# A triangular solve on one NeuronCore: the state of the block steps kept in natural layout instead of transposed

## The reference

```python
probs = jax.nn.softmax(logits + causal_mask, axis=-1)      # 16 heads of 8 dims, s = 512
L = jnp.eye(s) - jnp.tril(probs, -1)
rhs = jnp.diagonal(probs, axis1=-2, axis2=-1)[..., None] * v
A = jax.scipy.linalg.solve_triangular(L, rhs, lower=True)
return A.transpose(0, 2, 1, 3).reshape(b, s, 128) @ Wd.T + bd
```

## Time and profile before

| | |
|---|---|
| median of 3 runs | 1500.24 us (1497.93 to 1505.37) |
| profiled execution, span first to last instruction | 1507.1 us, 30851 instructions |
| mean granted TensorE clock, whole span | 0.883 |
| PE busy / DVE busy / ACT busy / POOL busy | 1237.4 / 1035.0 / 729.2 / 628.0 us |
| solve of the causal layer (first inverse to last copy) | 718.5 to 1181.0 us |

### The profile page before, as it was taken

One profiled execution on the slowest core, in us unless ns is written; L12 is line 12 of the kernel. 1 busy time (PEld: TensorE's weight loads), 2 busy tenths in 40 slices (PEclk: granted clock), 3 DMA queues, 4 the chain that ended last, 5 costly groups with the idle time before them and its releaser, 6 DMA issues. The chain is left out here.

```text
span 1507.1 us, 30851 instructions
## 1 busy us (share of the span) xinstructions
PE 1237.4 (82%) x11642; PEld 673.8 (45%) x11642; DVE 1035.0 (69%) x2290; ACT 729.2 (48%) x1596; POOL 628.0 (42%) x838
## 2 busy tenths in 40 slices
PE   6656677779999988538889988988988799999976
PEld 2212232222333337424666766666666333333276
DVE  6699999979888955457446646645632588988653
ACT  3834334317766675313524523533442166676754
POOL 2279888853424215314423423223332524351244
PEclk9878888869999998758889879978997599999988
DMA  5378833023224022441421231141120231331213
GB/s 166 145 274 320 298 139 140 20 67 87 55 65 122 13 82 63 100 86 23 88 38 25 45 74 28 21 100 18 18 51 10 67 79 31 97 89 45 81 48 88
DMA packets 137737, 128.41 MB, mean 85 GB/s; under 512 B 92007, under 2 KB 123559, under 8 KB 132202
## 3 DMA queue, kind: packets, MB, share of 16 engines
q1 hardware_dynamic: 129536, 118.56, 28.6%
q0 software_dynamic: 2496, 5.13, 1.1%
q10 hardware_dynamic: 5558, 2.76, 0.9%
HBM read 105.61 MB, written 38.62 MB: 96 GB/s over the span
## 5 line engine op out<-in xcount | busy, mean ns | idle before, releaser
L1393 DVE TENSOR_REDUCE f_row_min<-f_ps 128x1 f32<-128x512 f32 x512 | 323.9, 676 | 55.6 <-PE f_ps L1720 55.2
L1283 ACT ACTIVATE f_e<-f_ps 128x512 f32<-128x512 f32 x512 | 282.8, 602 | 126.4 <-PE f_ps L1740 122.5
L1720 PE MATMUL f_ps<-f_operands 72*128 72x512 bf16 x512 | 205.4, 410 | 26.4 <-DMA f_operands<-k_scr 15.4
L1740 PE MATMUL f_ps<-f_operands 75*128 75x512 bf16 x512 | 189.5, 380 | 2.6 <-ACT f_e L1283 2.1
L790 PE MATMUL m_ps<-m_shared,sb_ident 128*128 128x512 f32 x256 | 136.8, 683 | 58.1 <-DVE m_shared L630 58.0
L363 POOL TENSOR_TENSOR m_drive<-m_du,m_ring 128x1024 f32<-128x1024 f32 x64 | 149.7, 2352 | 56.2 <-DVE m_ps L622 37.6
L495 ACT ACTIVATE m_ps<-m_delta,m_A 128x511 f32<-128x511 f32 x128 | 83.0, 681 | 131.7 <-DVE m_ps L622 109.0
L1751 PE MATMUL f_ps<-f_e,f_v_op 128*32 128x512 f32 x1024 | 136.4, 604 | 2.1 <-ACT f_e L1283 1.4
L2714 DVE TENSOR_TENSOR d_aT<-d_ps,d_aT 128x16 f32<-128x16 f32 x224 | 37.9, 169 | 140.9 <-PE d_ps L2892 140.7
L1720 PEld LDWEIGHTS f_ps<-f_operands 72*128 72x128 bf16 x512 | 51.3, 101 | 181.2 <-DVE f_row_min L1393 127.3
L2545 DVE TENSOR_REDUCE d_row_min<-d_ps 128x1 f32<-128x384 f32 (+3 forms) x176 | 106.3, 634 | 35.9 <-PE d_ps L2786 34.7
(11 more groups left out here) (298 smaller groups left out, 2345.3 us busy)
## 6 DMA issues: line engine op xcount, KB each, us to landing
m_ring<-bc_scr SPq DMA_DIRECT2D x32, 1024.0 KB, 5.4
f_rows_scr<-blank SPq DMA_DIRECT2D x2, 8707.5 KB, 30.8
f_wall<-f_wall SPq DMA_DIRECT2D x16, 578.0 KB
f_operands<-q_scr SPq DMA_DIRECT2D x32, 288.0 KB
f_operands<-k_scr SPq DMA_DIRECT2D x96, 96.0 KB
d_q_op<-q_scr SPq DMA_DIRECT2D x6, 576.0 KB
d_k_op<-k_scr SPq DMA_DIRECT2D x18, 192.0 KB
f_operands<-f_rows_scr SPq DMA_DIRECT2D x46, 64.5 KB, 1.8
```

The costliest lines, as they stand in the source:

```text
L1283: nc.scalar.activation(e_sb[:, n % 3, hh, :], ps[:, SCORE[(b * UNITS + u) % SCORE_BANKS], :], ACT.Exp, scale=SCALE).then_inc(s["e_out"], 1)
L1393: nc.vector.tensor_reduce(row_min[:, b % 2, u // TPB, u % TPB:u % TPB + 1], ps[:, MAXQ[(b * UNITS + u) % MAX_BANKS], :], AX.X, ALU.max, ne ...
L1720: nc.tensor.matmul(ps[:, MAXQ[n % MAX_BANKS], :], q_op(b, QK)[:, hd, t * P:(t + 1) * P], k_op(b, QK)[:, hd, :], start=True, stop=True).the ...
L1740: nc.tensor.matmul(ps[:, SCORE[n % SCORE_BANKS], :], k_op(b, QKS)[:, hd, t * P:(t + 1) * P], q_op(b, QKS)[:, hd, :], start=True, stop=True ...
```

## The change

The state of the solve stays in natural layout, in `a_all`, through all steps. Each product now has the mixing block as stationary operand (32 columns of `mT`, tokens) and the state of one head as moving operand (8 columns), so that it comes out in natural layout, 32 tokens by 8 dimensions for each head, and VectorE adds it straight to `a_all`. Since an operand must start at a multiple of 32 partitions, blocks go in pairs: an even k brings to both blocks of a pair all that lies before the pair, an odd k the first block's contribution to the second, and a column of zeros and ones (`second`) masks the first block in the add. The transposes and copies between steps go; one transpose and copy of each half after the inverse stays (`natural`). For the output, ScalarE gathers the 16 heads into `a_flat`, PE transposes it once, ScalarE copies it to `a_out`, and one product by the unpadded weights replaces two by the padded ones; this happens at h = 0, 1 and 3. `multiplied` leaves out the first 16 of 128 columns of a head. Semaphore counts, zero sets and the column layout follow. The core of the diff:

```diff
-PADDED = NH * HEAD_COLS + 2 * HD
+PADDED = HD + NH * HEAD_COLS
...
-        a_nat = sb("a_nat", [P, PADDED])
         a_all = sb("a_all", [P, TPB, PADDED])
         gT = sb("gT", [P, 2, P])
-        aT = sb("aT", [P, 2, 2, P])
+        aT = sb("aT", [P, 2, P])
+        a_flat = sb("a_flat", [P, NH, HD])
+        a_out = sb("a_out", [P, 2, P])
...
+        def own_dims(t, hd):
+            c = HD + hd * HEAD_COLS
+            return t[:, c:c + HD]
         def of_head(t, hd):
-            return t[:, hd * HEAD_COLS:(hd + 1) * HEAD_COLS]
+            c = HD + hd * HEAD_COLS - hd // GROUP % 2 * HD
+            return t[:, c:c + HEAD_COLS]
...
+        def token_group(k):
+            return slice(k // 2 * 2 * BLK, (k // 2 + 1) * 2 * BLK)
+        def step_cols(half, rows):
+            return ps[rows, STEP[half], 0:NH // 2 * HD].rearrange("p (h d) -> p h d", d=HD)
...
-                    nc.scalar.copy(mT[:, n % 2, i * GROUP:(i + 1) * GROUP, :].rearrange("p h i -> p (h i)"),
-                                   act_bank("mt", n, i)).then_inc(s["act_out"], 1)
+                    nc.scalar.copy(mT[:, n % 2, i * GROUP:(i + 1) * GROUP, BLK:P],
+                                   act_bank("mt", n, i).rearrange("p (h i) -> p h i", h=GROUP)[:, :, BLK:P]).then_inc(s["act_out"], 1)
+                def flattened(n):
+                    act.wait_ge(s["at_sb"], 2 * BLKS * (n + 1))
+                    if n >= 1:
+                        act.wait_ge(s["act_out"], in_act("turned_out", n - 1))
+                    nc.scalar.copy(a_flat[:, :, :], every_own(a_all[:, n % TPB, :])).then_inc(s["flat_out"], 1)
+                def turned_out(n):
+                    act.wait_ge(s["act_ps"], in_act("turned_out", n))
+                    if n >= 2:
+                        act.wait_ge(s["dve_ps"], in_dve("output", n - 2))
+                    nc.scalar.copy(a_out[:, n % 2, :], act_bank("turned_out", n)[:, 0:P]).then_inc(s["act_out"], 1)
...
                 def beside(n, h):
+                    if n >= 1 and h == 0:
+                        flattened(n - 1)
+                    if n >= 1 and h == 1:
+                        turned_out(n - 1)
...
-                def turned(n, half, k):
-                    act.wait_ge(s["an_ps"], 2 * (n * BLKS + k) + half + 1)
-                    out = a_all[:, n % TPB, :] if k == TURNS else a_nat[:, :]
-                    nc.scalar.copy(own_cols(out, half), turned_cols(half)).then_inc(s["an_sb"], 1)
+                def turned(n, half):
+                    act.wait_ge(s["an_ps"], 2 * n + half + 1)
+                    nc.scalar.copy(by_group(own_cols(a_all[:, n % TPB, :], half)), turned_cols(half)).then_inc(s["an_sb"], 1)
                 for n in range(-LEAD, TILES_N):
                     if n == 0:
-                        act.wait_ge(s["set"], 4)
-                        act.wait_ge(s["zero_set"], 2)
+                        act.wait_ge(s["zero_set"], 3)
                     if n >= 0:
-                        turned(n, 0, 0)
-                        turned(n, 1, 0)
-                    for k in range(1, BLKS):
-                        beside(n, 2 * (k - 1))
-                        if n >= 0:
-                            turned(n, 0, k)
-                        beside(n, 2 * (k - 1) + 1)
-                        if n >= 0:
-                            turned(n, 1, k)
+                        turned(n, 0)
+                        turned(n, 1)
+                    for h in range(HOOKS):
+                        beside(n, h)
+                flattened(TILES_N - 1)
+                turned_out(TILES_N - 1)
...
-                    if n >= 1 and h == 0:
+                    if n >= 1 and h == 3:
                         add_output(n - 1)
...
-                        nc.vector.tensor_copy(aT[:, n % 2, half, :], step_bank(half)).then_inc(s["at_sb"], 1)
-                    dve.wait_ge(s["at_sb"], 2 * BLKS * n + 2)
+                        nc.vector.tensor_copy(aT[:, half, :], step_bank(half)).then_inc(s["at_sb"], 1)
                 def added(n, half, k):
-                    own = slice(k * BLK, (k + 1) * BLK)
+                    rows = token_group(k)
+                    held = own_cols(a_all[rows, n % TPB, :], half)
                     dve.wait_ge(s["at_ps"], 2 * (n * BLKS + k) + half + 1)
-                    nc.vector.tensor_tensor(aT[:, n % 2, half, own], ps[:, STEP[half], own], aT[:, n % 2, half, own],
-                                            ALU.add).then_inc(s["at_sb"], 1)
+                    if k % 2 == 0:
+                        nc.vector.tensor_tensor(held, step_cols(half, rows), held, ALU.add).then_inc(s["at_sb"], 1)
+                    else:
+                        nc.vector.scalar_tensor_tensor(out=held, in0=step_cols(half, rows), scalar=vec(core, "second")[rows, :],
+                                                       in1=held, op0=ALU.mult, op1=ALU.add).then_inc(s["at_sb"], 1)
...
-                        last = nc.tensor.matmul(bank[:, hh * P:(hh + 1) * P], e_nat[:, n % 3, hd, :], xT[:, n % 2, hd, :],
+                        last = nc.tensor.matmul(bank[:, hh * P + BLK:(hh + 1) * P], e_nat[:, n % 3, hd, :], xT[:, n % 2, hd, BLK:P],
...
-                    if n >= 1 and h == 0:
+                    if n >= 1 and h == 1:
+                        turn_out(n - 1)
+                    if n >= 1 and h == 3:
                         output(n - 1)
...
-                def side_by_side(half, lhs, rhs, rows, cols, done):
-                    for gl in range(2):
-                        for hh in range(GROUP):
-                            hd = head(half, gl, hh)
-                            last = nc.tensor.matmul(ps[hh * HEAD_COLS:(hh + 1) * HEAD_COLS, STEP[half], cols],
-                                                    of_head(lhs[rows, :], hd), rhs(hd), start=(gl == 0), stop=(gl == 1))
-                    last.then_inc(done, 1)
                 def turn_half(half, src, done):
                     nc.tensor.transpose(turn_bank(half), src[:, half, :], core.ident[:, :]).then_inc(done, 1)
+                def turn_out(n):
+                    pe.wait_ge(s["flat_out"], n + 1)
+                    nc.tensor.transpose(act_free("turned_out", n)[:, 0:P], a_flat[:, :, :].rearrange("p h d -> p (h d)"),
+                                        core.ident[:, :]).then_inc(s["act_ps"], 1)
                 def output(n):
-                    bank = dve_free("output", n)
-                    for half in range(2):
-                        last = nc.tensor.matmul(bank[:, 0:P], aT[:, n % 2, half, :], w["d_wd"][:, half, :],
-                                                start=(half == 0), stop=(half == 1))
-                    last.then_inc(s["dve_ps"], 1)
+                    pe.wait_ge(s["act_out"], in_act("turned_out", n))
+                    nc.tensor.matmul(dve_free("output", n)[:, 0:P], a_out[:, n % 2, :], w["d_wd"],
+                                     start=True, stop=True).then_inc(s["dve_ps"], 1)
...
                 def from_earlier(n, half):
                     t = n % TPB
-                    pe.wait_ge(s["an_sb"], 2 * BLKS * n - 1 + half)
+                    pe.wait_ge(s["at_sb"], 2 * BLKS * n - 1 + half)
...
+                def natural(n, half):
+                    pe.wait_ge(s["at_sb"], 2 * BLKS * n + half + 1)
+                    turn_half(half, aT, s["an_ps"])
                 def product(n, half, k):
-                    pe.wait_ge(s["an_sb"], 2 * (n * BLKS + k - 1) + half + 1)
-                    own = slice(k * BLK, (k + 1) * BLK)
-                    rows = slice(0, k * BLK)
-                    side_by_side(half, a_nat[:, :], lambda hd: mT[rows, n % 2, hd, own], rows, own, s["at_ps"])
-                def turned(n, half, k):
-                    pe.wait_ge(s["at_sb"], 2 * (n * BLKS + k) + half + 1)
-                    if n >= 1 and k == 0:
-                        pe.wait_ge(s["an_sb"], 2 * BLKS * n - 1 + half)
-                    turn_half(half, aT[:, n % 2], s["an_ps"])
+                    if k == 1:
+                        pe.wait_ge(s["an_sb"], 2 * n + half + 1)
+                    else:
+                        pe.wait_ge(s["at_sb"], 2 * (n * BLKS + k - 1) + half + 1)
+                    own = token_group(k)
+                    rows = slice(0, own.start) if k % 2 == 0 else slice(own.start, own.start + BLK)
+                    for gl in range(2):
+                        for hh in range(GROUP):
+                            c = (gl * GROUP + hh) * HD
+                            last = nc.tensor.matmul(ps[own, STEP[half], c:c + HD], mT[rows, n % 2, head(half, gl, hh), own],
+                                                    own_dims(a_all[rows, n % TPB, :], head(half, gl, hh)), start=True, stop=True)
+                    last.then_inc(s["at_ps"], 1)
                 for n in range(-LEAD, TILES_N):
                     if n == 0:
-                        pe.wait_ge(s["set"], 4)
-                        pe.wait_ge(s["zero_set"], 2)
```

(19 more changed lines are left out.)

40 lines of the change are left out of this document (21 added, 19 removed).

## The result

The changed kernel takes 1629.6 us (median of 4 runs, 1624.0 to 1634.3) against 1500.7 us for the kernel before: ratio 1.083, 95% interval 1.078 to 1.088. The sign was forecast, the size not: +129 us instead of +58, and outside the range.

The account below looks back on a forecast made before the run. PE was taken to bound the solve: products +89, transposes -30, waits -21, adds +3, output -3 make +38; the clock's +20 gives +58 on the 1500.2 us median, 1558 us. Range 1495 to 1615 us.

Parts of the forecast that it names:

- Products, +89: In the solve, 16 passes of each product follow one another in one strip: +89 us, bounds +81 and +115.
- Transposes, -30: On PE in the solve, 208 of 256 transposes go: -30 us.
- Waits, -21: PE's waits for the add and ScalarE's copy, 31 us, go with the solve's loop; a third left: -21 us.
- adds +3: VectorE's adds on 32 partitions take 225 against 169 ns, mostly hidden under PE: +3 us (0 to 12.5).
- output -3: Output needs 32 passes less, 4 us, against 1 us for gather, transpose and copy at the end: -3 us.
- Sum +38: All work and wait terms of the change together, clock left out: +38 us, ends -8 and +94.
- The clock, +20: PE's granted clock in the solve falls in more tiles, 60 us more at half clock: +20 us.
- A: Rival: the clock stays as it was, +38, 1538 us; chance 0.27.
- B: Rival: faster, 40% of the longer products' 89 us hides where VectorE is slower, 1473 us; chance 0.18.
- C: Rival: nothing to see, low product price and all waits gone, or transposes never in PE's way, 1503 us; chance 0.10.

Follow-up runs that it names:

- run 1: The kernel before, with all 16 passes of a product writing the same 32 PSUM partitions: 1579.9 us, ratio 1.050.
- run 4: The changed kernel with one 128x128 transpose, result unused, before each product after the first step (192 in all): 1602.9 us, ratio 1.067.
- run 5: The changed kernel with every add of the solve plain, without the mask at odd steps: 1621.7 us, ratio 1.076.
- run 10: The kernel before with two unused 384-column matmuls behind a half step's transpose, where the solve showed half clock: 1502.7 us, ratio 0.999.
- 15: The kernel before, a product's 16 passes in one strip, two unused 384-column matmuls behind half-step transposes at half-clock places: 1574.0 us, ratio 1.044.
- run 14: The changed kernel with 8 of each product's 16 passes and four unused 384-column matmuls before each product after the first steps: 1551.2 us, ratio 1.029.

## Why the forecast was wrong, by its own steps

**Products, +89: right as PE's own time, too high for what shows.** 0.030 us a pass and a spread of 0.45 us were taken, at half clock 0.81; measured 0.50/15 = 0.033, 0.50 and 0.82. That 32 stationary columns cost a quarter of 128 held. But run 1 shows +64 us for the solve where the term says 89, as 0.07 of the 0.36 us of each product hides beside the other work of the tile. So the term is at least 25 us too high.

**Transposes, -30: right as work, wrong as an effect.** The fourth tile of run 4 at nearly full clock took 31.2 us, 2.1 above 29.1 for 12 transposes, 0.175 us each; 0.145 was taken. But with them in, the kernel is 27 us faster. My own sentence that the change "takes full-width transposes out" named the cause, and the clock's term then had no amount worked out from it.

**Waits, -21, adds +3, output -3: not far off, as far as the runs show.** PE's idle time in the solve went from 51.5 to 23.5 us, 28 less. The products' loads now wait 5.9 us for the adds (3.4 for the masked, 2.5 for the plain). The fourth tile had hardly any of these waits (PE idle 1.5 of 26.9 us), and there nothing of it shows: 26.9 + 4.1 for the serial passes (run 1) - 13 x 0.175 for the 16 transposes of a tile that became 3 is 28.7, against 29.1. The masked form took 280 ns, above the 225 by which I had bounded it, and run 5 puts that at 5 us at most.

**Sum +38: not borne out.** The fourth tile shows +2.2 us, which would be 16 x 2.2 = +35 if every tile were like it. The third tiles are not. Tile 6 (the third of the second batch) at full clock, in the kernel before and in the changed one with two, four and six fillers (2, 12, 13):

```profile
909.70:939.40 29.70, 25.41 (x489) 18.70 (x490) 21.59 (x70) 10.96 (x31) 12.06 (x33) 1.00 0.18 25
```

```profile
944.60:976.30 31.70, 30.94 (x497) 23.68 (x498) 24.93 (x70) 8.61 (x19) 11.94 (x33) 1.00 0.17 24
```

```profile
933.90:969.00 35.10, 34.48 (x519) 26.07 (x522) 24.90 (x70) 8.61 (x19) 12.00 (x33) 1.00 0.15 21
```

```profile
974.10:1013.20 39.10, 38.42 (x544) 28.52 (x547) 24.76 (x70) 8.61 (x19) 12.08 (x33) 1.00 0.15 21
```

With the fillers taken off (3.9 us for each two before a product), the changed tile takes 27 to 28 us, 2 us less than before: PE was idle 4.3 us there, and that wait is gone. With +64 for the products and PE's -28 us of idle time in the place of +89 and -21, the forecast's own sum is 38 - 25 - 7 = +6 us, an estimate. So the sum of work and waits was most likely too high, by some 30 us, and without that the total would have missed by still more.

**The clock, +20: the step that failed.** It read "I take 60 us more at half clock". The runs show 282. The price was sized well, if somewhat low: +20 for 60 us is 0.33 a us, and the fourth tile shows 0.39 to 0.44, near the 0.5 that half the speed can cost. I had reckoned it where the loop of product, add and wait is in charge (20% of a step), and most of the solve is PE-bound. The amount was chosen, not worked out, between my own bounds of -20 and +110, and the choice had no row behind it, though rows 10 showed exactly the stretch that the change makes more of. (The lower bound leaves out its own 58 products of 0.25 us, and would be about -35.) At 0.39 to 0.44 us, the 282 us are worth 110 to 124. So my bound for all the time at half clock, +110, came out nearer than my value.

How the 123 us divide over the whole solve is bounded, not settled. If every tile were like the fourth, the clock would have 123 - 35 = 88 us. By the solve as a whole, 551 us with four fillers less their 123 leaves 428 us for the changed kernel at nearly full clock. Of the kernel before, run 10 comes nearest to that: 454 us less what its 256 fillers cost, which is nothing at the least, 27 at 0.107 us each and 41 at 0.16, so 413 to 454. Work and waits then lie between a gain of 26 us and a loss of 15, and the clock has 108 to 149 us. These estimates take the first two fillers of a product at the price of the later ones, which no run shows; run 4's price of the clock does without that. By each of them the clock has the larger part.

**Rivals.** A (the clock stays, 1538) fell with the clock. The Trainium skill's rule on idle gaps (TensorE: Matmul & The Clock Gate, HAM oscillation), by which A would have won, is contradicted by the fall at 862 us above. B (the products hide behind VectorE) was nearer than its time, 1473, lets it look. A product shows 0.29 us (runs 1 and 15), under the 0.36 at which I had let B decide, but a fifth of it hides and not 40%, and run 14 shows 47 of 59 us for the passes at full clock. What B gains in waits the clock took, and more. C's two ways, a low price of the products or transposes that are not in PE's way, meet 0.033 us a pass and 0.175 us a transpose.

**The signs I had named:** 16 passes in 0.6 to 0.7 us (0.67), 48 transposes of the solve (32 and 16 for the output, and the 24 of the entering state that were there before), granted clock under 0.87 (0.65), the solve at about 520 us (584), a step of the last tile no shorter than before (1.80 against 1.50 at half clock, where I had expected no change at full). The solve's length missed by what the clock cost. Neither sign of being wrong came: the passes do not overlap again, and the waits for VectorE in the solve shrank by 28 us at PE's weight loads and by 17 at its matmuls, under the 40 named.

## What to carry to other kernels

When a change takes wide matmuls out of a PE-bound stretch (one where PE's own work sets the time) or narrows them, price the granted clock as a term of its own, between "as now" and "half throughout", and take the side that the nearest stretch of the same kind shows; then test it by adding wide matmuls without effect, since a kernel that gets faster from more work has a clock problem. A layout that saves a transpose but puts all its small matmuls on the same 32 output partitions pays in serial passes: count the strips first, and see whether the reader of the result can take it from other partitions. And full clock has its price: a filler pays only where it costs less than the half clock that it takes away. Two before each product bought 22 us in the changed kernel, four nothing that is clear of noise, and in the kernel before they cost about what they gave.

## What was not expected of the hardware

- PE work can shorten the time: +192 transposes -27 us, +384 matmuls of 384 bf16 columns -22 us, 128 columns instead of 112 perhaps -14 us (the intervals touch).
- Doubling small passes that overlap in four strips did not lower the clock (97 us at half against 121); putting the same passes one after another in one strip did (161). The changed kernel, which has one strip and lacks the transposes, was at half clock far longer (403, and 265 with them back).
- The start-to-start time of these passes is 0.033 us in one strip at full clock but 0.055 at half (0.82/15): 1.65 times, not 2.
- VectorE reads 32 PSUM partitions and adds into 32 other SBUF partitions in one instruction; the natural layout in two strips rests on it.
